# A relational graph layer whose first gather sums raw rows for four of sixteen relations

## The reference, cut to what matters

```python
deg = jnp.zeros((R, N), dtype=x.dtype).at[edge_type, dst].add(1.0)
deg = jnp.maximum(deg, 1.0)
h_all = jnp.einsum('nd,rdo->rno', x, W_r)
msg = h_all[edge_type, src] / deg[edge_type, dst][:, None]
agg = jax.ops.segment_sum(msg, dst, num_segments=N)
return agg + x @ W0_w.T + W0_b
```

## Time and profile before

| What | Value |
|---|---|
| Device time, median of 3 runs | 4071.96 us (4071.23 to 4074.68) |
| Profiled execution, span from first to last instruction | 4443.8 us; a time of its own beside the span is not listed |
| Granted clock of PE, mean over the span | 0.855 |
| Relation stage | about 38 to 794 us of the span |
| First gather (`stage_first`) | about 802 to 2019 us |
| Experts | about 2050 to 2520 us |
| Second gather and what follows it | about 2526 to 3715 us |
| LSTM | about 3720 us to the end |

### The profile page before, as it was taken

How to read it: one execution, slowest core, us unless ns; L and a number is a source line. 1 busy time by engine, 2 the same in 40 slices (tenths; PEclk the granted TensorE clock), 3 DMA queues, 4 the chain that set the end, 5 groups by cost and what they waited for, 6 DMA issues and landing times. The chain is left out here.

```text
span 4443.8 us, 59668 instructions
## 1 busy us (share of the span) xinstructions
PE 3422.0 (77%) x18753; PEld 2613.4 (59%) x18753; DVE 1898.4 (43%) x5881; ACT 912.0 (21%) x2407; POOL 1686.3 (38%) x1769
## 2 busy tenths in 40 slices
PE   7999999455567666667999554566667779999996
PEld 3444444354556555565666444445555557999996
DVE  4555300133334444454555421223334445544687
ACT  2333333000000111112333200000000002444554
POOL 1000000566666666653222366666666660000000
PEclk9999999677777777778999766777888889999998
DMA  4333444333444545553333323333444444433333
GB/s 148 149 149 149 154 168 164 116 107 110 124 122 144 161 134 148 150 150 108 116 113 110 109 86 94 107 116 122 126 138 146 152 154 147 153 126 119 110 109 113
DMA packets 246926, 580.34 MB, mean 131 GB/s; under 512 B 45059, under 2 KB 130588, under 8 KB 232783
## 3 DMA queue, kind: packets, MB, share of 16 engines
q1 hardware_dynamic: 158816, 334.44, 21.9%
q0 software_dynamic: 85344, 238.92, 18.3%
q10 hardware_dynamic: 2448, 3.15, 0.2%
HBM read 384.29 MB, written 191.42 MB: 130 GB/s over the span
## 5 line engine op out<-in xcount | busy, mean ns | idle before, releaser
L1676 POOL DMA_INDIRECT b_msg<-scratch_gx,k_src_row x782 | 770.6, 985 | 385.2 <-issue 220.0
L941 POOL DMA_INDIRECT a_msg<-scratch_hrel,k_rel_row x782 | 755.1, 966 | 424.1 <-issue 214.8
L717 PE MATMUL r_psm<-k_w,r_xnT 128*128 128x512 f32 x1568 | 696.4, 599 | 10.4 <-ACT k_slab L681 9.5
L1019 PE MATMUL a_ps<-a_hit,a_msg 128*128 128x128 f32 x3128 | 556.5, 343 | 170.6 <-issue 112.9
L1727 PE MATMUL b_ps<-b_hit,b_msg 128*128 128x128 f32 x3128 | 481.2, 317 | 197.3 <-issue 117.9
L1019 PEld LDWEIGHTS a_ps<-a_hit,a_msg 128*128 128x128 f32 x3128 | 501.3, 248 | 209.6 <-issue 137.4
L1727 PEld LDWEIGHTS b_ps<-b_hit,b_msg 128*128 128x128 f32 x3128 | 462.8, 230 | 246.4 <-issue 148.4
L2130 PE MATMUL l_psg<-k_hall,k_whhT 128*128 128x125 f32 x4640 | 550.7, 277 | 5.2 <-DVE k_hall L2256 5.2
L2130 PEld LDWEIGHTS l_psg<-k_hall,k_whhT 128*128 128x128 f32 x4640 | 538.4, 193 | 5.7 <-DVE k_hall L2256 5.7
L717 PEld LDWEIGHTS r_psm<-k_w,r_xnT 128*128 128x128 f32 x1568 | 294.2, 192 | 356.0 <-issue 342.5
L1831 DVE TENSOR_TENSOR k_accT<-k_accT,b_ps 128x256 f32 x196 | 82.6, 422 | 654.2 <-remote 476.0
(11 more groups left out here) (290 smaller groups left out, 4200.4 us busy)
## 6 DMA issues: line engine op xcount, KB each, us to landing
l_xr<-scratch_xrow SPq DMA_DIRECT2D x146, 512.0 KB
scratch_hrel<-k_slab SPq DMA_DIRECT2D x50, 1024.0 KB
scratch_hrel<-r_hst SPq DMA_DIRECT2D x48, 1024.0 KB
scratch_xrow<-n_xs SPq DMA_DIRECT2D x50, 512.0 KB
a_typ<-scratch_typ SPq DMA_DIRECT2D x196, 96.0 KB
a_msg<-scratch_hrel,k_rel_row POOLq DMA_INDIRECT x782
b_msg<-scratch_gx,k_src_row POOLq DMA_INDIRECT x782
n_xb<-scratch_gx SPq DMA_DIRECT2D x48, 256.0 KB
```

The lines of the kernel that those rows point to most:

```text
L717: mm = pe.matmul(psm[:, c % 4], xnT[:, u, kk], k.w[:, kk, c * 512:(c + 1) * 512], start=(kk == 0), stop=(kk == 1))
L941: pool.indirect_dma_start(msg[:, q, j], None, table, bass.IndirectOffsetOnAxis(ap=rows_of[:, g, j:j + 1].bitcast(U32), axis=0)).then_inc(s ...
L1019: mm = pe.matmul(ps[:, u, kk, 0:WIN], msg[:, g % SL, j, kk * P:(kk + 1) * P], hit[:, u, j], start=(j == 0), stop=(j == pieces(g)[-1]))
L1676: pool.indirect_dma_start(msg[:, q, j], None, rows_of, bass.IndirectOffsetOnAxis(ap=k.src_row[:, g, j:j + 1].bitcast(U32), axis=0)).then_i ...
```

## The change

The table keeps 12 products a node and, as a thirteenth block, the normalized row itself (`R1` = 12). An edge of relations 12 to 15 gathers that row. In the first gather the hits have five slots: slot 0 for messages of the first 12 relations, slots 1 to 4 for raw rows of the other four. 128 columns hold five slots of at most 24 targets, so the windows become narrower: units of four, two or one piece of 128 edges (`cut_units`), 512 in all, each with an address, an add and a frame of its own. `acc` holds ten stretches (two halves times five slots) of 640 targets as a ring, which ACT clears tile by tile (`wipe`) and whose overhang VectorE folds back (`spill`). `turn_sums` multiplies the four extra sums with their W_r. ACT copies the window of `thirds` for each unit into a frame (`framed`), so that PE loads no address. VectorE loads the addresses of a group at the head of its slot (`places`), and likewise seven addresses before a tile's norm in the relation stage. POOL makes the units' windows in the relation stage (`windows`); if an edge lies outside, `again` builds a full table of 16 products for the loop over windows. Cut to its core:

```diff
+SUMMED = 4
+RING = 5
+def width(k, p, m):
+    nodes = place(k, (p + m) * P) - place(k, p * P)
+    return -(-int(1000 * (nodes + 2 + 4.2 * nodes / (P * m) ** 0.5)) // 2000) * 2
...
+        m = next(m for m in (4, 2, 1) if p % m == 0 and width(k, p, m) <= WIN // (SUMMED + 1))
...
+                            leads = bass.AP(tensor=dst.tensor, offset=0, ap=[[0, 1], [P, k.NPC]])
+                            sp.dma_start(k.at[:, 0:k.NPC], leads).then_inc(s_first, 16)
...
-                v.wait_ge(s_first, 16)
+                v.wait_ge(s_first, 32)
...
-    NC = R * D // 512
+            NC = (R if full else k.R1) * D // 512
...
+                            if z == C1 and not full:
+                                sp.dma_start(k.hrel[bass.ds(t * P, P), k.R1 * D:(k.R1 + 1) * D],
+                                             xn[:, u]).then_inc(s_i[u], 16)
...
+                    if counted:
+                        windows(pool)
                     pool.memset(k.accT[:], 0.0).then_inc(S["z"], 1)
...
+                        if not full:
+                            rest(k, v, s_i[s % 2], 16 * (2 * i + s // 2) + 16)
                         ln.rows(v, t, xt[:, s], xn[:, s % 2])
...
+                                at = places(XR * i + s)
                                 ahead(i, s)
-                                adds(XR * i + s)
+                                adds(XR * i + s, at)
...
+        with nc.If(nc.values_load(k.late[0:1, 0:1], min_val=0, max_val=1) > 0):
+            clear(k, [*S.values(), *s_x, ln.s_step, ln.s_var, ln.s_std, *deg.sems])
+            again()
+        nc.all_engine_barrier()
...
+                        for r in range(SUMMED):
+                            sp.dma_start(wq[:, :, r * D:(r + 1) * D],
+                                         W_r[k.R1 + r].rearrange("(k p) o -> p k o", p=P)).then_inc(S["wq"], 16)
...
-                        at = pe.value_load(k.base[0:1, g:g + 1], min_val=0, max_val=k.NP - WIN)
...
+                        for n in units_in(g):
+                            p, m, w = k.units[n]
+                            for j in pieces_of(n):
+                                mm = pe.matmul(psw[:, u, j * 64:j * 64 + w], hotT[:, u, j * P:(j + 1) * P],
+                                               frame[:, g % FR, p % PER, 0:w], start=True, stop=True)
...
+                        for f in range(k.fills_to[g], k.fills_to[g + 1]):
+                            if f >= 2:
+                                pe.wait_ge(s_add, k.fills[f - 2][-1] + 1)
...
+                        for r in range(SUMMED if along else 0):
+                            for kk in range(2):
+                                pe.matmul(psa[:, 0:D], acc[:, kk * NS + 1 + r, lands(t)], wq[:, kk, r * D:(r + 1) * D],
+                                          start=False, stop=False, skip_group_check=True)
...
+                    def framed(g):
+                        if g >= FR:
+                            act.wait_ge(s_wt, g - FR + 1)
+                        for n in units_in(g):
+                            p, m, w = k.units[n]
+                            at = act.value_load(k.at[0:1, p:p + 1], min_val=0, max_val=k.NP - k.widest)
+                            ins = act.copy(frame[:, g % FR, p % PER, 0:w], k.thirds[:, bass.ds(at, w)])
...
+                            ins = v.scalar_tensor_tensor(
+                                out=slotted(hit[:, u, j, 0:NS * w]), in0=slotted(k.iota[:, 0:NS * w]),
+                                scalar=k.cell[:, g, j:j + 1],
...
+                    def places(g):
+                        return [v.value_load(k.at_ring[0:1, k.units[n][0]:k.units[n][0] + 1], min_val=0, max_val=k.RL - 1)
+                                for n in units_in(g)]
...
+                            for i, n in enumerate(k.fills[f]):
+                                w = k.units[n][2]
+                                if n:
+                                    v.wait_ge(s_add, n)
+                                to = acc[:, :, bass.ds(at[n - k.upto[g]], w)].rearrange("p (h s) w -> p h s w", h=2)
...
+                                v.tensor_tensor(to, to, of, ALU.add).then_inc(s_add, 1)
...
                     for g in slots:
+                        if along and g < NG:
+                            at = places(g)
```

More of the change, by code:

```diff
@@ new lines, in again, with _ @@
+        def again():
+            with nc.Block(no_gpsimd_drain=True) as block:
+                @block.vector
+                def _(v):
+                    link = Chain(v, S["re"])
+                    link(v.tensor_copy(table(0), edge(k.src_row)))
+                    link(v.scalar_tensor_tensor(out=table(0), in0=table(0), scalar=R / 2.0, in1=edge(k.typf),
+                                                op0=ALU.mult, op1=ALU.add))
+                    link(v.tensor_copy(edge(k.rel_row), table(0)))
+                @block.sync
+                def _(sp):
+                    for s in range(XR):
+                        sp.dma_start(xt[:, s], x[s * P:(s + 1) * P]).then_inc(s_x[s], 16)
+            run(False, True)
@@ L565, in run @@
+        def run(counted, full=False):
+            NC = (R if full else k.R1) * D // 512
+            C1 = (NC + 1) // 2
+            to = k.hfull if full else k.hrel
+            hst = (k.slab, k.slab if full else second)
             with nc.Block(no_gpsimd_drain=True) as block:
@@ L634, in builds, with places, adds @@
                                 deg.build(v, t * PT + c, c)
-                        def adds(t):
+                        def places(t):
+                            return [v.value_load(k.base[0:1, bass.ds(t * PT + c, 1)], min_val=0, max_val=k.NP - WIN)
+                                    for c in range(PT)]
+                        def adds(t, at):
                             for c in range(PT):
-                                deg.add(v, t * PT + c, c, None)
+                                deg.add(v, t * PT + c, c, at[c])
                         builds(0)
@@ L709, in turn, with tile @@
                         mm.then_inc(S["tp"], 1)
-                    def tile(t, u, more, groups):
+                    def tile(t, s, more, groups):
+                        u = s % 2
                         rest(k, pe, S["xt"], t + 2)
@@ L780, in stage_first @@
     s_s = [k.sem(f"g_s{u}") for u in range(SR)]
+    s_q = [k.sem(f"g_q{u}") for u in range(XQ)]
     k.s_slab = k.sem("g_slab")
@@ L923, in tiles @@
             ended = lambda g: [b for b, (lo, hi) in enumerate(batches) if begin[hi - 1] == g]
+            sums_at = lambda f, i, kk: banks[:, f % 2, (2 * i + kk) * WIN:(2 * i + kk + 1) * WIN]
+            units_in = lambda g: range(k.upto[g], k.upto[g + 1])
+            pieces_of = lambda n: range(k.units[n][0] % PER, k.units[n][0] % PER + k.units[n][1])
+            if along:
+                assert all(begin[k.wiped[g] - 1] <= g - 2 for g in range(NG) if k.wiped[g])
             with nc.Block(no_gpsimd_drain=True) as block:
@@ L1266, in _ @@
                     if along:
+                        v.memset(hit[:].rearrange("p u j w -> p (u j w)"), 0.0).then_inc(S["hz"], 1)
+                        v.wait_ge(S["hz"], 1)
                         hot(0)
```

303 lines of the change are left out of this document (225 added, 78 removed).

## The result

The changed kernel takes 4142.07 us (median of four runs), the kernel before 4073.32 beside it: a ratio of 1.0164, 95% interval 1.0148 to 1.018. It is slower by some 69 us, where +12 was forecast. The result lies inside the whole range of 3960 to 4190 us, but 12 us above the forecast's own range of 4040 to 4130, and at the price of none of the rivals.

What follows compares the result with a forecast made beforehand. It took PE to bound the relation stage and POOL the gathers, with VectorE becoming the bound late in the first gather. -168 + 8 + 3 + 5 + 164 = +12 us, 4084; own range 4040 to 4130, whole range 3960 to 4190.

Steps and rivals of the forecast that it cites:

- +240: First gather: upper bound of VectorE's excess over POOL, with 0.65 between adds and 0.7 us a load.
- Relation products, -168: Relation stage: 8 fewer PE records a tile save 3.43 us in each of 49 tiles, -168 us.
- Lead tiles, +8: First 28 tiles, counting degrees: VectorE's seven address loads run mostly under the builds; +8 us, bounds 0 and +64.
- Stores of the normalized rows, 0: Relation stage: norm waits for the extra store, but the DMA share was taken to show it has landed; no cost.
- First loads, +3: Start of the kernel: the larger first-edge load delays the SP queue with the weights behind it; +3 us (0 to 4).
- Flag, branch and barrier, +5: Between relation stage and first gather: the new branch on the flag with a barrier costs +5 us (0 to 9).
- POOL's window tables, 0: Relation stage: some 85 small POOL operations cost nothing while they end before PE; without that cover some 60 us.
- First gather, VectorE's address loads: Last 89.5 groups: four exposed loads, 0.62 us each, 2.48 a group, help make VectorE the bound; whole excess +164 us.
- Rival 1: First gather: address loads run under other work, POOL stays the bound, 3920 us (half hidden 3973); chance 0.13.
- First gather, PE, 0: First gather: PE's sums, weighing and new products of a tile stay hidden under VectorE's time; no cost.
- 5.1, under VectorE's 6.86, so nothing: First gather: PE's work a group at the full clock level is 5.1 us, below VectorE's 6.86, so it adds nothing.
- Rival 3: First gather: PE falls to the half clock level and becomes the bound at 8.2 us a group, 4204 us; chance 0.13.

Runs made afterwards that it cites:

- run 11: Changed kernel with unchecked loads behind the hits and in the lead tiles, weighing two groups ahead, four buffers of normalized rows: 3952.41 us, ratio 0.9712 to the kernel before.
- Run 6: Changed kernel with address loads unchecked and behind the slot's four hits, and unchecked in the lead tiles as well: 4026.38 us.
- Run 10: Changed kernel with four buffers of normalized rows in the relation stage instead of two, a semaphore each for their stores: 4121.42 us.
- run 8: As Run 6, with PE weighing two groups ahead, right after its sums: 3964.94 us.
- run 2: Changed kernel with the places of the first gather's adds fixed at build time, so VectorE loads no addresses there (sums wrong): 3982.72 us.
- 5: Changed kernel with the first gather's address loads still at the slot's head but without their bounds check: 4066.06 us.
- Run 7: Changed kernel with fixed places for the adds and without the 16 products a tile of the gathered sums: 3931.88 us.
- run 3: Changed kernel without PE's 16 matmul records a tile that multiply gathered sums with the four weight blocks: 4117.57 us.

## Why the prediction came out as it did

The side came out as forecast, but it was hardly a call: the prediction gave 0.47 to slower and 0.44 to faster. The mechanism named as likeliest is there; the size was off by four fifths: +61.4 by the profiles for +12. The terms that had a price were near. Two terms that were put at nothing were not nothing, and all the larger errors lie on one side, so nothing cancelled: 28 us in the first gather, 17 in the stores, 8 in the lead tiles. One bound can't be had from its terms: 2.7 + 3 x 0.65 + 0.15 + 4 x 0.7 is 7.6 us a group, +230 and not +240.

**Relation products, -168: right.** With the two obstacles below out of the way (run 11) the relation stage is 753.3 - 589.1 = 164.2 us shorter.

**Lead tiles, +8: 16 us.** The 28 tiles gained 79.9 of 96. "VectorE's sequencer has nothing to wait for after it has issued the builds" was too hopeful: the seven loads of a tile begin late in its builds. Its loads on VectorE's sequencer, and then the last build and the next statistics on the timeline:

```profile
L779 DVEq TENSOR_LOAD <-k_base x7: 298/304/348, 251.5 to 255.7; - x7
```

```profile
254.41 0.22 DVE L434 TENSOR_TENSOR d_hot<-k_iota,k_typf 128x64 bf16<-128x64 f32 x1
...
256.86 0.43 DVE L145 BATCH_NORM_STATS2 ln_stats<-k_xt 128x6 f32<-128x256 f32 x1 [2.23 <-issue]
...
272.31 0.43 DVE L145 BATCH_NORM_STATS2 ln_stats<-k_xt 128x6 f32<-128x256 f32 x1 [5.16 <-issue]
```

The first load starts 3.1 us before the builds end at 254.63, and from one load to the next pass 0.69 us; so 3.1 us of seven loads are hidden, not the 5.2 that all builds last, and 2.23 show. In the next tile nothing is hidden: it is the first of a pass of the loop over four tiles, its first load starts at 267.10, when the last build has begun, and 5.16 us show; from 113 to 325 us it goes so in every fourth tile (5.0 to 5.2 us). Run 6 took the checks away and the tiles became PE's alone, 18.5 us shorter. Here the trace does show VectorE running its queue while its sequencer loads; the Trainium skill (Perfetto Trace Analysis, "DVE / Act Engine Instruction") says that the sequencer hands an instruction to a queue and goes on to the next, and these rows agree.

**Stores of the normalized rows, 0: 17 us.** The step "the stage's DMA share says that it has landed" failed. The share (0.43 in the earlier trace rows) tells how busy the DMA engines are; what counted was the store's place on the SP queue, behind 15 transfers that wait for VectorE. The prediction had itself written that norm waits for the store with the builds behind it, and did not ask what stands ahead of the store. Run 10 shows the mechanism (the gap falls from 25.8 to 11.5 us, 9.6 before) and gives back 9.0 of the 17 (13.4 beside run 8's edits); what makes the rest, the new wait of 2.4 us and the longer busy time among it, is open.

**First loads, +3: 6.1 us.** VectorE ends its part of the loads at 32.53 for 28.92 before, 3.6 us. The other 2.5 are the same new wait once more: at the start of the relation stage the first normalization waits for the transfer that primes its semaphore.

```profile
40.28 0.43 DVE L145 BATCH_NORM_STATS2 ln_stats<-k_xt 128x6 f32<-128x256 f32 x1 [7.75 <-DMA scratch_primed<-k_zero]
```

**Flag, branch and barrier, +5: 4.5. POOL's window tables, 0: right**; POOL's 65.86 us in the second stretch end under PE's products, and the seam grew by no more than the branch.

**First gather, VectorE's address loads: right in kind.** The loads hold the late groups, as 2 and 5 show, and cost up to 151 us (124 if the adds' address steps are taken off), where the whole excess was put at 164. From one load to the next pass 0.67 us in the mean, where 0.62 was put; the median is 0.62. Rival 1 falls; what it would have taken is to be seen in 5 and 8.

**First gather, PE, 0: 18 us beside the loads, 41 to 47 without them.** The step "5.1, under VectorE's 6.86, so nothing" failed. It compared the sum of PE's work in a group with VectorE's, as if they ran side by side. They don't: the products of a tile come whole, in one slot, and the weighing that VectorE's next hits need stood behind them. On PE's timeline of the changed kernel:

```profile
1606.52 3.62 PE L1224 MATMUL g_psa<-k_accT 128*128 128x256 f32 x16
...
1610.93 0.26 PE L1191 MATMUL a_psw<-a_frame,a_hotT 48*128 48x22 bf16 x4
```

(The weighing, like the counting of degrees, is in bf16, not in float32 as the opening says of all matrix work.) Run 7 beside run 2 puts the products at 47.4 us once the loads are gone, run 3 at 17.7 while they stand. So the +192.3 in the gather and its tail can be split as 151.0 for the loads and 41.3 for the rest (from 2 to the kernel before), or as 17.7 for the products and 174.6 for the rest: each covers a part of the other. Either way the prediction's 164 left out 28. That the order is a large part of it run 8 shows for the kernel with unchecked loads behind the hits (56.3 us); that it is all of it is not shown.

Rival 3, PE at the half level, was not the cause: the granted clock of the stretch is 0.82 after and 0.81 before, from the first group with four units to the experts 0.82 in both, and taking PE's 16 records away gains 17.7 us instead of 100. By the rule that the prediction weighed (the Trainium skill, TensorE: Matmul & The Clock Gate, "The HAM clock gate") a PE that waits could have fallen to the half level; the granted clock shows no such fall from before to after. Whether the half level adds to PE's lateness in the tile slots was not tried by itself.

That the tail behind the last gather is 54.5 us longer belongs to the same terms: POOL is up to seven groups ahead, so VectorE's lag shows first as a longer tail (run 2: all of it) and only then as waits of POOL.

## What to carry to other kernels

Price a new wait by what stands ahead of the awaited thing on its queue, not by how busy the queue is, and price new work on an engine by who is behind it in that engine's order, not by its sum beside another engine's sum. While an address is loaded into a register, nothing new is issued to the engine (here VectorE stood 2.87 us at four loads): put the load behind work that is already queued, and look at how much of it is a check of bounds (here 0.26 of 0.67 us). When a bound goes, measure the next edit again: the same reordering was worth 6.5 us behind one bound and 56.3 without it.

## What the runs showed of the hardware

Address loads were longer in the mean where another engine loaded at the same time. From 1360 to 1809 us of the changed kernel VectorE's 149 reads that met none of ScalarE's lasted 0.31 us in the mean, the 100 that did 0.40, and single ones up to 0.95. A long read meets more of them by its length alone; but the 56 that began while ScalarE was already reading also lasted 0.41 in the mean, with a median of 0.31, so a few long ones make the difference. That ScalarE's reads are the cause is not shown: no run took them out, and in the counting tiles, where ScalarE loads none, single reads of VectorE reach 0.92. If they are, ScalarE's frames, which the prediction put at nothing, have a small price on VectorE.

Dropping the check of the bounds leaves the bare read: 0.41 us from load to load for 0.67 in the mean. That alone, in the first gather, brought the changed kernel back to the time of the one before (4066.06 us beside 4072.24 on the same chip).
